# Conditional residual kernel: the LoRA part of the bias summed on VectorE, its vector turned to a row by two small DMAs

## The reference

```
y   = x + x @ W0[b].T + bias0      W0[b] = mask * sum_g cond[b,g] * weight[g]
out = y + y @ W1[b].T + bias1      W1[b] = base + 2 * sum_g cond[b,g] * B[g] @ A[g]
```

```
bias[b] = bias0 + bias1 + base @ bias0 + 2 * sum_g cond[b,g] * B[g] @ (A[g] @ bias0)
```

## Time and profile before

| | |
|---|---|
| time, median of 3 runs | 56.83 us (56.14 to 57.04) |
| profiled execution, its own time | 56.49 us |
| its span on the engines | 54.7 us |
| TensorE busy | 50.9 us, 93% of the span |
| VectorE busy | 39.9 us, 73% |
| ScalarE busy | 31.7 us, 58% |
| GpSimd busy | 30.6 us, 56% |
| read from and written to HBM | 7.54 MB and 4.19 MB |

### The profile page before, as it was taken

How to read it: one execution, slowest core, us unless ns; L and a number is a source line. 1 busy time by engine, 2 the same in 40 slices (tenths; PEclk the granted TensorE clock), 3 DMA queues, 4 the chain that set the end, 5 groups by cost and what they waited for, 6 DMA issues and landing times.

```text
span 54.7 us, 971 instructions
## 1 busy us (share of the span) xinstructions
PE 50.9 (93%) x330; PEld 46.1 (84%) x330; DVE 39.9 (73%) x64; ACT 31.7 (58%) x53; POOL 30.6 (56%) x30
## 2 busy tenths in 40 slices
PE   2999999999999999999999999999999999999900
PEld 2989999999998978998898889889889889888800
DVE  0049996989799996999999893789819949805030
ACT  1939944404935399539609961992992940840800
POOL 4004349585990099998945999999998100000000
PEclk9999999999999999999999999999999999999999
DMA  0698999999999997000820280073063064059582
GB/s 0 162 381 230 368 379 393 424 416 413 419 395 407 422 395 291 33 0 0 306 84 0 78 318 0 0 271 118 0 247 136 0 226 157 0 205 369 193 288 96
DMA packets 5476, 11.79 MB, mean 216 GB/s; under 512 B 608, under 2 KB 1376, under 8 KB 5472
## 3 DMA queue, kind: packets, MB, share of 16 engines
q1 hardware_dynamic: 5184, 11.35, 55.5%
q10 hardware_dynamic: 288, 0.39, 2.0%
HBM read 7.54 MB, written 4.19 MB: 215 GB/s over the span
## 4 chain that ended last, share of the span: by engine, by line
PE 93%; DVE 1%; issue 0%
PE ps_out L463 13%; PE ps_out L532 13%; PE ps_out L467 13%; PE ps_out L471 13%; PE ps_merge L463 8%; PE ps_merge L467 8%; PE ps_merge L471 8%; PE ps_merge L573 6%; PE ps_lora L477 4%; PE ps_lora L463 2%; PE ps_lora L467 2%; PE ps_lora L471 2%; DVE out_sb L454 1%; PE ps_out L594 1%; DVE warm L322 0%
## 5 line engine op out<-in xcount | busy, mean ns | idle before, releaser
L193 POOL TENSOR_TENSOR W_lo<-W,W_hi 128x512 fp32r<-128x512 f32 x8 | 12.2, 1523 | 3.8 <-ACT W_hi L242 3.7
L360 DVE TENSOR_TENSOR x_lo<-x_sb,x_hi 128x1024 fp32r<-128x1024 f32 x8 | 11.7, 1466 | 0.0
L463 PE MATMUL ps_out<-x_hi,M_hi 128*128 128x512 f32 (+1 forms) x32 | 9.8, 388 | 0.0
L255 ACT ACTIVATE M_hi<-ps_merge 128x512 fp32r<-128x512 f32 x8 | 4.8, 595 | 8.5 <-PE ps_merge L471 8.5
L467 PE MATMUL ps_out<-x_lo,M_hi 128*128 128x512 f32 (+1 forms) x32 | 9.7, 384 | 0.0
L471 PE MATMUL ps_out<-x_hi,M_lo 128*128 128x512 f32 (+1 forms) x32 | 9.7, 383 | 0.0
L199 POOL TENSOR_TENSOR W_lo<-W,W_hi 128x512 fp32r<-128x512 f32 x6 | 9.4, 1574 | 0.4 <-ACT W_hi L248 0.3
L262 ACT ACTIVATE x_hi<-x_sb 128x1024 fp32r<-128x1024 f32 x8 | 8.5, 1057 | 0.0
L375 DVE TENSOR_SCALAR out_sb<-ps_out,bias_sb 128x512 f32<-128x512 f32 x7 | 5.2, 748 | 4.0 <-PE ps_out L471 3.9
L532 PE MATMUL ps_out<-packs_sb 128*128 128x128 f32 x64 | 7.3, 275 | 0.0
L532 PEld LDWEIGHTS ps_out<-packs_sb 128*128 128x128 f32 x64 | 7.2, 192 | 0.0
(11 more groups left out here) (65 smaller groups left out, 73.7 us busy)
## 6 DMA issues: line engine op xcount, KB each, us to landing
x_sb<-xT_dram SPq DMA_DIRECT2D x8, 512.0 KB, 10.8
outT_dram<-out_sb SPq DMA_DIRECT2D x15, 256.0 KB, 2.3
packs_sb<-packs_dram SPq DMA_DIRECT2D x7, 288.0 KB, 5.6
rows_sb<-rows_dram SPq DMA_DIRECT2D x1, 384.0 KB, 7.3
base_sb<-base_dram ACTq DMA_DIRECT2D x1, 256.0 KB, 3.5
outT_dram<-out_sb SPq DMA_DIRECT2D x2, 128.0 KB, 1.8
packs_sb<-head_dram SPq DMA_DIRECT2D x1, 192.0 KB, 3.3
packs_sb<-rest_dram SPq DMA_DIRECT2D x1, 160.0 KB, 4.6
```

What stands on the lines that cost most here:

```text
L193: pool.tensor_tensor(W1_lo[:, b % W1BUF], W1[:, b % W1BUF], W1_hi[:, b % W1BUF].bitcast(f32), ALU.subtract).then_inc(w1lo_done, 1)
L360: nc.vector.tensor_tensor(x_lo[:, b % XBUF], x_sb[:, b], x_hi[:, b % XBUF].bitcast(f32), ALU.subtract).then_inc(xlo_done, 1)
L463: nc.tensor.matmul(out, hi_l, hi_r, start=(n == 0), stop=False)
```

## The change

The TensorE matmul of the LoRA part (L594), with `low_bias` as it was and the semaphores `low_done` and `bias_mm`, is gone. In its place:

- `rows` is wider: B with outputs on partitions (two halves of 128 values of (g, r)) and all 64 numbers of cond on every partition are added to it, 320 f32 more on each partition.
- The dot product of A moves ahead of `m_lo(0)`, and `b_lo(7)` behind `m_lo(0)`. SyncE, behind the loads, waits for that dot product, writes the 128 numbers A_bias0 to a DRAM vector (128 pieces of 4 bytes), waits for that to land (`written`), and reads the vector back to each of the 128 partitions (128 pieces of 512 bytes, `turned`). The output stores stand behind both in SyncE's program.
- VectorE multiplies that row with B and 2, sums over r, multiplies with cond, sums over g, and adds the rest as before: four operations ahead of the two of L439.
- VectorE's `split_x_lo(2)` moves ahead of this chain and `m_lo(2)` behind it, ahead of `out1(0)`.
- The second half of `apply(1)` waits for the two dot products of base (which read the row in bank 3), no longer for `bias_done`.

```diff
--- before.py
+++ after.py
@@ -35,7 +35,11 @@
     WARM = 28
     assert packs.shape == (NQ - 1, P, PACKW)
 
+    column = nc.dram_tensor("A_bias0_dram", (P,), f32, kind="Internal").ap()
     OB0, OB1, OA, OBT = NB, NB + NT, NB + 2 * NT, NB + 2 * NT + C
+    OBR = (NT + 1) * C
+    OCR = OBR + NT * P
+    ROWS = OCR + NB * NG
     cut = MIXW + C
 
     with ExitStack() as ctx:
@@ -65,9 +69,12 @@
         A_er = lora_sb[:, OA:OA + C]
         B_er = lora_sb[:, OBT:OBT + C]
         base_sb = sb("base_sb", [P, NT, C])
-        rows_sb = sb("rows_sb", [P, NT + 1, C])
-        base_rows = rows_sb[:, 0:NT, :]
-        bias0_row = rows_sb[:, NT, :]
+        rows_sb = sb("rows_sb", [P, ROWS])
+        base_rows = rows_sb[:, 0:NT * C].rearrange("p (j c) -> p j c", j=NT)
+        bias0_row = rows_sb[:, NT * C:OBR]
+
+        B_rows = rows_sb[:, OBR:OCR].rearrange("p (j r) -> p j r", j=NT)
+        cond_row = rows_sb[:, OCR:ROWS].rearrange("p (b g) -> p b g", b=NB)
         x_sb = sb("x_sb", [P, NB, NT, TOK])
 
         warm = sb("warm", [P, 128], bf16)
@@ -77,7 +84,11 @@
         A_bias0 = sb("A_bias0", [P, 1])
         bias_sum = sb("bias_sum", [P, NT])
         base_bias0 = sb("base_bias0", [P, NT])
-        low_bias = sb("low_bias", [P, NB])
+        A_bias0_row = sb("A_bias0_row", [P, P])
+        B_products = sb("B_products", [P, NT, P])
+        expert_bias = sb("expert_bias", [P, NT, NG])
+        cond_products = sb("cond_products", [P, NT, NB, NG])
+        low_bias = sb("low_bias", [P, NT, NB])
         bias_sb = sb("bias_sb", [P, NT, NB])
         A_hi = sb("A_hi", [P, C], f32r)
         A_lo = sb("A_lo", [P, C], f32r)
@@ -110,7 +121,6 @@
         ps_last = ps_lora[0][:, 0, :]
 
 
-        ps_bias = ps_out[3][:, 0:NT * NB].rearrange("p (j b) -> p j b", j=NT)
         ps_row = ps_out[3][:, C:2 * C]
 
 
@@ -122,8 +132,9 @@
         x_in = [sem(f"x_in{b}") for b in range(NB)]
 
         warm_set, ident_zero, ident_done = sem("warm_set"), sem("ident_zero"), sem("ident_done")
-        base_done, dots_done, low_done, fixed_done = sem("base_done"), sem("dots_done"), sem("low_done"), sem("fixed_done")
-        row_done, bias_mm, bias_done, bhi_done, blo_done = sem("row_done"), sem("bias_mm"), sem("bias_done"), sem("bhi_done"), sem("blo_done")
+        base_done, dots_done, sums_done, fixed_done = sem("base_done"), sem("dots_done"), sem("sums_done"), sem("fixed_done")
+        row_done, written, turned = sem("row_done"), sem("written"), sem("turned")
+        bias_done, bhi_done, blo_done = sem("bias_done"), sem("bhi_done"), sem("blo_done")
 
         ahi_done, alo_done = sem("ahi_done"), sem("alo_done")
         lora_mm, w1_done, w1hi_done, w1lo_done = sem("lora_mm"), sem("w1_done"), sem("w1hi_done"), sem("w1lo_done")
@@ -154,7 +165,13 @@
             for b in range(NB):
                 sp.dma_start(x_sb[:, b], xT[b].rearrange("p (j n) -> p j n", j=NT)).then_inc(x_in[b], 16)
                 if b == 0:
-                    sp.dma_start(rows_sb[:, :, :], rows.rearrange("p (j c) -> p j c", j=NT + 1)).then_inc(rows_in, 16)
+                    sp.dma_start(rows_sb[:, :], rows).then_inc(rows_in, 16)
+
+
+            sp.wait_ge(dots_done, 1)
+            sp.dma_start(column.unsqueeze(1), A_bias0[:, :]).then_inc(written, 16)
+            sp.wait_ge(written, 16)
+            sp.dma_start(A_bias0_row[:, :], column.partition_broadcast(P)).then_inc(turned, 16)
 
             for b in range(NB):
                 for j in range(NT):
@@ -415,34 +432,45 @@
             ramp_low(0)
             ramp_low(1)
             split_x_lo(0)
-            b_lo(7)
-            m_lo(0)
-
             dve.wait_ge(row_done, 1)
             dve.wait_ge(rows_in, 16)
             dot(A_er, A_bias0[:, :]).then_inc(dots_done, 1)
-            dve.wait_ge(dots_done, 1)
-            nc.vector.tensor_scalar(low_bias[:, :], cond_er, A_bias0[:, :], SCALING,
-                                    ALU.mult, ALU.mult).then_inc(low_done, 1)
-
+            m_lo(0)
+            b_lo(7)
             nc.vector.tensor_tensor(bias_sum[:, :], bias0, bias1, ALU.add).then_inc(fixed_done, 1)
             m_lo(1)
             split_x_lo(1)
 
-            dve.wait_ge(bias_mm, 1)
+            dve.wait_ge(dots_done, 1)
             for j in range(NT):
                 dve.wait_ge(dots_done, 1 + j)
                 dot(base_rows[:, j, :], base_bias0[:, j:j + 1]).then_inc(dots_done, 1)
+            split_x_lo(2)
+
+            dve.wait_ge(turned, 16)
+            nc.vector.scalar_tensor_tensor(out=B_products[:, :, :], in0=A_bias0_row[:, :].unsqueeze(1).to_broadcast([P, NT, P]),
+                                           scalar=SCALING, in1=B_rows, op0=ALU.mult, op1=ALU.mult).then_inc(sums_done, 1)
+            dve.wait_ge(sums_done, 1)
+            nc.vector.tensor_reduce(expert_bias[:, :, :], B_products[:, :, :].rearrange("p j (g r) -> p j g r", g=NG),
+                                    mybir.AxisListType.X, ALU.add).then_inc(sums_done, 1)
+            dve.wait_ge(sums_done, 2)
+            nc.vector.tensor_tensor(cond_products[:, :, :, :], expert_bias[:, :, :].unsqueeze(2).to_broadcast([P, NT, NB, NG]),
+                                    cond_row.unsqueeze(1).to_broadcast([P, NT, NB, NG]), ALU.mult).then_inc(sums_done, 1)
+            dve.wait_ge(sums_done, 3)
+            nc.vector.tensor_reduce(low_bias[:, :, :], cond_products[:, :, :, :],
+                                    mybir.AxisListType.X, ALU.add).then_inc(sums_done, 1)
             dve.wait_ge(dots_done, 1 + NT)
             dve.wait_ge(fixed_done, 1)
+            dve.wait_ge(sums_done, 4)
             for j in range(NT):
-                last = nc.vector.tensor_scalar(bias_sb[:, j, :], ps_bias[:, j, :], base_bias0[:, j:j + 1],
+                last = nc.vector.tensor_scalar(bias_sb[:, j, :], low_bias[:, j, :], base_bias0[:, j:j + 1],
                                                bias_sum[:, j:j + 1], ALU.add, ALU.add)
             last.then_inc(bias_done, 1)
             dve.wait_ge(bias_done, 1)
+            m_lo(2)
             for b in range(1, NB):
                 out1(b - 1)
-                if b + 1 < NB:
+                if 1 < b < NB - 1:
                     split_x_lo(b + 1)
                     m_lo(b + 1)
                 if b == 1 or b == 3:
@@ -557,7 +585,8 @@
                     if b >= 2:
                         pe.wait_ge(out_done[i], b - 1)
                     if b == 1 and i == 1:
-                        pe.wait_ge(bias_done, 1)
+
+                        pe.wait_ge(dots_done, 1 + NT)
                     cols = slice(i * P, (i + 1) * P)
                     whole = b < NB - 1 or i < NT - 1
                     for n in [slice(0, TOK)] if whole else [slice(0, TOK // 2), slice(TOK // 2, TOK)]:
@@ -589,11 +618,6 @@
 
             pe.wait_ge(w0_done, NQ)
             apply(0)
-            pe.wait_ge(low_done, 1)
-            for i in range(NT):
-                mm = nc.tensor.matmul(ps_bias[:, i, :], B_er[:, i * P:(i + 1) * P], low_bias[:, :],
-                                      start=True, stop=True)
-            mm.then_inc(bias_mm, 1)
             for b in range(1, NB):
                 if b + 1 < NB:
                     merge(b + 1)
@@ -637,7 +661,8 @@
     lora = np.concatenate([np.repeat(cond.T, R, axis=0), halves(bias0[:, None]), halves(bias1[:, None]),
                            A_er, Bs.transpose(0, 2, 1).reshape(G * R, C)], axis=1)
 
-    rows = np.concatenate([halves(base), np.broadcast_to(bias0, (P, C))], axis=1)
+    rows = np.concatenate([halves(base), np.broadcast_to(bias0, (P, C)), halves(Bs.transpose(1, 0, 2)),
+                           np.broadcast_to(cond.reshape(-1), (P, NB * G))], axis=1)
     xT = np.ascontiguousarray(x.transpose(0, 2, 1).reshape(NB, NT, P, TOK).transpose(0, 2, 1, 3).reshape(NB, P, NT * TOK))
     cut = P + C
     first = P + packs.shape[1] // NQ - P // NQ
```

## The result

| | before | after |
|---|---|---|
| time, median of 6 runs | 56.69 us (56.14 to 57.04) | 65.68 us (64.85 to 66.22) |
| profiled execution, its own time | 56.49 us | 65.68 us |
| span | 54.7 us | 63.9 us |

What follows compares the result with a forecast made beforehand. TensorE, busy 93% of the span, was taken as the bound. Its stand made merge(4) +1.1 us late, w1_lo(4) made that +1.7, the 0.45 gain included: 56.49 + 1.7 = 58.2 us, range 56.6 to 59.4.

Steps and rivals of the forecast that it cites:

- The matmuls removed, 0.45 us: On TensorE, 0.36 us for the four L594 matmuls plus 0.09 in merge(2)'s first pair; a gain of 0.45 us.
- x_lo(2) held by GpSimd, ending at 26.1: On VectorE from 23.98, held by GpSimd's w0_lo(3): about 2.1 us, ending at 26.1; undisturbed 25.2.
- The two DMAs, `turned` at 26.4 (25.8 to 27.6): On SyncE's queue: write lands behind x's last load at 24.3 to 24.5, read takes 2.0; row back at 26.4.
- slow detour: Rival, 15%: 4-byte pieces or the read take longer through DRAM, `turned` after 27.1, end at 58.9 to 60.2 us.
- fixed cost of about 2.0 us a transfer: Alternative estimate for the two DMAs: both through near 23.5 from 19.3, making the sum 0.3 us less.
- The chain on VectorE, 2.13 us: The bias operations on VectorE from 26.4: 2.13 us (1.8 to 2.5), so bias_done at 28.5, before 24.46.
- TensorE's stand, 1.55 us: TensorE, ready for apply(2) at 27.73, waits for out0(0) until 29.3: a stand of 1.55 us.
- The clock, a rival at 5%: Rival, 5%: TensorE's stand lowers its clock from 2.4 to 1.2 GHz until merge(4); 59 to 62 us.
- w1_lo(4) holding merge(4), +0.6 us: GpSimd's w1_lo(4) ends at 34.0 and holds TensorE's merge(4), about 0.6 us more idle: +1.7 instead of +1.1.

Runs made afterwards that it cites:

- e3: The changed kernel with the loads of x of samples 4 to 7 issued behind the two small DMAs; 65.68 us.
- e15: The changed kernel, complete, with 16-byte pieces, loads of x of samples 4 to 7 behind the small DMAs, and VectorE's program reordered; 57.71 us, ratio 1.024.
- e1: The changed kernel without its two small DMAs, bias0's first 128 values in place of the row (LoRA part not computed); 58.39 us, ratio 1.042.
- e2: The changed kernel with merge(3) computed six times in place of once, to keep TensorE busy; 63.79 us, ratio 1.135.
- e4: The changed kernel with the 4-byte pieces written 512 bytes apart in DRAM and an unwritten row read back; 60.74 us.
- e13: The changed kernel with the 4-byte pieces written 16 bytes apart in DRAM and an unwritten row read back; 61.10 us.
- e8: The changed kernel with the 4-byte pieces written to a column of SBUF and an unwritten row read back; 58.96 us.
- e14: The changed kernel, complete, with A_bias0 as first column of a tile 4 wide, so 16-byte pieces side by side; 59.70 us, ratio 1.055.

## Why the prediction was wrong

- **The matmuls removed, 0.45 us**: right. From apply(0)'s start to merge(2)'s it is 2.82 us instead of 3.16 (apply(0) began at 19.31 before, 19.23 now), and merge(2)'s first pair takes 0.23 instead of 0.33.
- **x_lo(2) held by GpSimd, ending at 26.1**: right, 2.21 us and 25.98.
- **The two DMAs, `turned` at 26.4 (25.8 to 27.6)**: this step failed. The write was to land 0.4 us behind the last load of x; it landed 3.8 us behind (27.6). The read was to take 2.0 and took 4.7. The vector was 5.9 us late against the forecast. I put the write behind the queue, which is right for every other kind of piece (0.1 to 0.2 us behind x) but not for this one, whose pieces took 7.4 us in an empty queue too (e3); and in the middle of the range I took nothing for the pieces, since the rows at hand, transfers of 128 KB, have no small piece in them. The read was sized from the same rows, which do not read pieces so written; the rival "slow detour" (15%) named the mechanism but ended at 60.2, since I scaled 0.7 us for the pieces from nothing in the trace. The estimate by the Trainium skill's fixed cost of about 2.0 us a transfer (page "DMA: Bandwidth & Descriptors", section "Anatomy of one DMA", which is about transfers that GpSimd issues; here SyncE does) was further off still, but its figure is fair for the two transfers without the crowd: 1.4 us for the write in an empty queue (e15), 2.6 to 3.1 for reads of 64 KB from other bytes. The same page's section "Specifications" says that DMAs below 512 bytes are done by read-modify-write; behind the full queue the runs show no price for that at 4 bytes as long as the pieces are not adjacent.
- **The chain on VectorE, 2.13 us**: right, 2.14, the reductions at 0.42 and 0.29 us like the multiplies of the same sizes. In part luck: GpSimd stood still beside it; in e1, where it did not, the same chain took 2.67 us (25.61 to 28.28).
- **TensorE's stand, 1.55 us**: the mechanism right (out0(0) behind bias_done), the size from the failed step: 7.61.
- **The clock, a rival at 5%**: with a stand of 1.55 us it would have stayed full, as e1 with 1.68 us shows; with 7.61 it fell and apply(2) cost 1.92 us more, 1.3 net of the wait that this covers (next item).
- **w1_lo(4) holding merge(4), +0.6 us**: right in e1 and e2 (0.5 us); in the changed kernel the slow apply(2) covers it (w1_lo(4) ends at 40.03, merge(4) starts at 41.46).

The miss adds up: 58.2 forecast, +6.1 for the longer stand, +1.9 for the clock, -0.6 for the wait that it covered, is 65.6; measured 65.68.

## What to carry to other kernels

A DMA round trip that starts behind a full queue costs the queue or its own write, whichever ends later, and then the read, and a landing is priced by its pieces too, not only by its bytes: where the trace has no row with such pieces, leave the upper end open, or time the transfer by itself first. Turning a column to a row through DRAM is cheaper with 16-byte pieces, three quarters of them zeros (59.7 us), than with adjacent 4-byte ones (65.7 us), though four times the bytes come back. Before a matmul of 0.45 us is moved off TensorE, count what the new producer stands behind; here even a free row won nothing measurable.

## What was not expected of the hardware

- 128 adjacent pieces of 4 bytes written to DRAM landed 3.1 to 3.8 us behind the load ahead of them, and 7.4 us after issue in an empty queue (e3). 128 pieces of 4 bytes 8 or more bytes apart, 16-byte pieces side by side, and 4-byte pieces to SBUF landed 0.1 to 0.2 us behind that load. Dividing the adjacent ones in four groups 4 KB apart did not help.
- A read of the bytes so written took 4.0 to 4.7 us, where others of its size, also behind such a write, took 2.6 to 3.1.
- A stand of TensorE of 7.6 us left it at 1.2 GHz (granted clock 0.50 from 35.40 to 39.00). Stands of 3.1 (e4) and 3.6 us (e13) also brought work at 0.50; stands of 1.7 (e1), 2.4 (e8) and 3.0 us (e14) left the granted clock full.
